# Three starts of stages rearranged in a 15-stage vision tower: buffers cleared behind the gathers, maxima of q, k and v taken one pair later, the shared experts' weights loaded in the routing before them

## The chip, the cores and the metric

The kernel runs on one core of one Trainium2 chip. The metric is the device time of one execution in microseconds; 2848.2 is the median of three runs. A profile is one more execution, recorded by the hardware.

## The reference, cut to what matters

The model is a tower of four layers over 64 images of 36 tokens (2304 tokens of width 192, f32). Each layer is an attention-like block and a feed-forward block, each followed by a layer norm of `h + block(h)`. Three blocks matter here:

```python
def L2_attn(x, ...):                       # "spectral"
    z = causal_conv4(x @ W_mem)            # 4 taps: the token and the 3 before it
    k_val, s_raw = z[..., :192], z[..., 192:]
    q = x @ W_q
    p_w = exp(clip(score_scale * s_raw, -20, 20) - slopes * dist)
    phi = tanh(tanh_scale * k_val) * theta            # 192 x 4 angles
    sums = cumsum([p_w, k_val * p_w * cos(phi), k_val * p_w * sin(phi)])
    ...                                    # times q and w_int, per-head products, gate
    return y @ out_W

def L2_ffn(x, ...):                        # swiglu: 2 shared experts, 16 routed, top 2
    shared = mean_s(silu(x @ shared_wg[s]) * (x @ shared_wu[s]) @ shared_wd[s])
    w, idx = top_k(softmax(x @ gate_w.T), 2)
    routed = sum_e combine[:, e] * (silu(x @ wg[e]) * (x @ wu[e]) @ wd[e])
    return shared + routed

def L3_attn(x, w_in, w_out):               # quantised: fake_quant needs the largest |value| of a whole tensor
    q, k, v = split(x @ fake_quant(w_in).T)
    q, k, v = fake_quant(q), fake_quant(k), fake_quant(v)
    scores = fake_quant(q @ k.T / 4)
    attn = fake_quant(softmax(scores))
    ...
```

## The kernel before

The tokens are held as 22 tiles of 108 (three images each), two tiles to a pair, so most loops run over 11 pairs (`NP = 11`, `G = 2`). The state `h` stays in SBUF. The program is a row of 15 stages (`PARTS`). In a stage every engine runs its own instruction list, written out by hand, with semaphores between engines; at the end of a stage all engines meet. The order within a list is fixed, so an instruction that waits holds up all behind it on that engine.

**Loading ahead.** `Ahead` reserves the SBUF of a later stage's weights and puts their transfers on the list `cst["coming"]`. A stage that calls `load_ahead` issues the whole list on SP's queue. The reader calls `arrived`, which waits until all transfers that were ever issued in this way have come. `clear_before` clears the semaphores of the stage before, one instruction for each, on SP. The routing stage of the swiglu block (`rt_swiglu`, `make_route`) does not call `load_ahead`; the next stage, `stage_shared`, loads its own weights `w1[x]`, `w2[x]` first and then the list: the quantised stage's three small tensors and `w2swiglu`, the 9216 KB of the routed experts.

**stage_shared.** TensorE runs `rise(n)` (up-projections) and `fall(n)` (down-projection) for 2 x 11 pairs. `rise` waits for `s_w[x]`, the two transfers of expert `x`. GpSimd meanwhile scatters the rows of `h` for the routed experts with 44 indirect transfers.

**Combine.** The stage behind a routed block gathers each token's expert rows by indirect transfers and adds and normalises them. For pair `p`: `fetch(2p)`, `fetch(2p+1)` on GpSimd (two gathers each, a ring of 4 tile buffers), `take(p)` on VectorE (two adds and statistics for each tile), `power(p)` on GpSimd (1/sqrt of the variances, and the shift), `level(p)` on ScalarE.

**stage_spectral.** GpSimd clears `hs` (the transposed pair and its three shifted copies, the borders of which must be zero, and one row of ones for the gate's bias) and `zz`. `shifts(p)` makes the shifted copies, `angles(p)` the angles `phi`, `scales(p)` the weights `kw`, `sums(p)` the sums of products. ScalarE's first copy into `hs` waits for `s_fix` = 3, the third clearing. TensorE's `keys(0)` waits for `shifts(0)`. VectorE's `rotations(0, u)` waits for `scales(0)` and ScalarE's sines; `weighted(0)`, which feeds `scales(0)`, comes ahead of `take(2)` on VectorE.

**stage_quantised, first phase.** For each pair TensorE projects q, k and v, ScalarE does `turned(p + 1)`, `level(p + 2)`, `queries(p)`, `values(p)` in this order, and VectorE `take(p + 2)`, `keys(p)` (copies k out of PSUM) and `looks(p)`: the largest absolute value of `h`, then of q (waits for `queries(p)`), k and v. When all 11 pairs are through, the scales of q, k, v are made, and the scores follow. `sel` is a constant bf16 matrix built from the identity, first needed after the scores; `q3` is the scores' left operand, whose borders must be zero. GpSimd clears both after the first 8 gathers, and VectorE fills `sel` between `take(0)` and `take(1)`:

```python
C_.take(dve, 0)
dve.wait_ge(s_fix, 4)
for i in range(3):
    dve.tensor_copy(sel[:, i]..., ident[0:T, i * IMG:(i + 1) * IMG]...)
C_.take(dve, 1)
for p in range(NP):
    if p + 2 < NP:
        C_.take(dve, p + 2)
    keys(p)
    looks(p)
```

## Time and profile before

| what | value |
|---|---|
| median of three runs | 2848.2 us (2841.95 to 2851.45) |
| profiled execution | 2844.44 us, span of its instructions 2842.6 us |
| TensorE busy | 2283.0 us, 80% of the span; mean granted clock 0.853 |
| VectorE, ScalarE, GpSimd busy | 1468.1, 895.3, 893.9 us |
| DMA | 225.44 MB, mean 79 GB/s |
| spectral stage | from about 1250 to 1661 us |
| routing of swiglu, shared experts, routed experts | 1661 to 1713, 1713 to 1965, 1966 to 2324 us |
| quantised stage | 2325 to 2619 us |

The profile counts from the first instruction. An engine is busy while it runs an instruction; "idle before <-releaser" is the time that it stood still before one, and what it had waited for last. PE is TensorE, DVE VectorE, ACT ScalarE, POOL GpSimd; SPq is SyncE's queue, which issues transfers. The granted clock is the share of full speed that TensorE got (1.00 is 2.4 GHz, 0.50 is 1.2 GHz).

### The profile page before, as it was taken

How to read it: one execution, taken by the hardware profiler on the slowest of the kernel's cores; microseconds unless marked ns; L12 is line 12 of the kernel's file. 1: busy time of each engine (PE TensorE's matmuls, PEld its weight loads, DVE VectorE, ACT ScalarE, POOL GpSimd, SP SyncE). 2: the span in 40 equal slices, each digit the busy share in tenths (PEclk: the TensorE clock that was granted, in tenths of full speed). 3: DMA queues.
4: the chain of work that ended last, by engine and by line, in shares of the span. 5: the costliest groups of instructions: out<-in, count | busy, mean ns of one | idle time of the engine just before them, and what ended most of it. 6: DMA issues, size and time to landing. Idle time of an engine off the chain costs nothing. (4 is left out here: it accounts for less than half of the span.)

```text
span 2842.6 us, 47911 instructions
## 1 busy us (share of the span) xinstructions
PE 2283.0 (80%) x18049; PEld 2006.4 (71%) x18049; DVE 1468.1 (52%) x3564; ACT 895.3 (31%) x1923; POOL 893.9 (31%) x809
## 2 busy tenths in 40 slices
PE   7999975599699759956888967998999977553793
PEld 7888863477588649954666667998999966532692
DVE  2667766456577632237888852222442236846313
ACT  0333326423154213324454411111111113754112
POOL 0332325600110342245665406000111136443424
PEclk9989975599799769977999968999999988555696
DMA  9500000060000435530000006001666631000453
GB/s 258 169 1 1 1 1 18 12 201 2 1 2 2 142 103 173 176 95 15 10 10 5 1 2 244 1 1 75 214 213 213 208 124 41 1 1 2 168 176 90
DMA packets 127066, 225.44 MB, mean 79 GB/s; under 512 B 17201, under 2 KB 97645, under 8 KB 119798
## 3 DMA queue, kind: packets, MB, share of 16 engines
q1 hardware_dynamic: 116278, 204.09, 21.9%
q0 software_dynamic: 10560, 18.29, 2.2%
q8 instruction: 145, 2.38, 0.3%
q14 instruction: 83, 0.68, 0.1%
HBM read 169.29 MB, written 53.02 MB: 78 GB/s over the span
## 5 line engine op out<-in xcount | busy, mean ns | idle before, releaser
L2513 POOL COPY bl_swiglu_w<-ahead_w2swiglu_w 128x1152 f32 x53 | 60.7, 1148 | 478.0 <-PE psum L2557 275.4
L2539 PE MATMUL psum<-bl_swiglu_xt,bl_swiglu_w 128*128 128x128 f32 x1272 | 153.0, 277 | 4.6 <-DMA bl_swiglu_w<-in_swiglu_w 3.6
L2539 PEld LDWEIGHTS psum<-bl_swiglu_xt,bl_swiglu_w 128*128 128x128 f32 x1272 | 151.0, 194 | 5.2 <-DMA bl_swiglu_w<-in_swiglu_w 4.0
L2581 ACT ACTIVATE bl_swiglu_sg<-psum 128x384 f32<-128x384 f32 x106 | 52.0, 490 | 310.5 <-PE psum L2546 310.5
L2608 DVE COPY bl_swiglu_xt<-psum 128x256 f32<-128x256 f32 x53 | 22.5, 424 | 206.5 <-PE psum L2524 206.5
L2692 PE MATMUL psum<-tower_xT,shared_w 128*128 128x216 f32 x528 | 103.1, 353 | 18.9 <-DMA shared_w<-in_shared_w 18.9
L2593 ACT ACTIVATE bl_gelu_hid<-psum,bl_gelu_w 128x128 f32<-128x128 f32 x270 | 74.5, 375 | 124.4 <-PE psum L2546 124.4
L2692 PEld LDWEIGHTS psum<-tower_xT,shared_w 128*128 128x128 f32 x528 | 98.5, 195 | 19.7 <-DMA shared_w<-in_shared_w 19.1
L2557 PE MATMUL psum<-bl_swiglu_w,bl_swiglu_hid 128*128 128x192 f32 x636 | 112.1, 326 | 0.0
L2737 DVE TENSOR_TENSOR shared_hid<-shared_sg,psum 128x432 f32<-128x432 f32 x66 | 39.9, 604 | 134.1 <-ACT shared_sg L2728 128.6
L2513 POOL COPY bl_gelu_w<-ahead_w2gelu_w 128x1350 f32 x45 | 58.9, 1312 | 152.5 <-DVE bl_gelu_y L2628 137.2
L2036 POOL DMA_INDIRECT rows_in<-tower_h,tower_spots x66 | 65.3, 990 | 122.5 <-POOLq L2094 74.8
L2557 PEld LDWEIGHTS psum<-bl_swiglu_w,bl_swiglu_hid 128*128 128x128 f32 x636 | 102.1, 190 | 0.1
L2728 ACT ACTIVATE shared_sg<-psum 128x432 f32<-128x432 f32 x66 | 35.0, 530 | 207.3 <-PE psum L2699 207.3
L2605 DVE TENSOR_SCALAR bl_gelu_xt<-psum,bl_gelu_gb 128x128 f32<-128x128 f32 x90 | 32.8, 406 | 121.5 <-PE psum L2524 121.5
L2557 PE MATMUL psum<-bl_gelu_w,bl_gelu_hid 128*128 128x192 f32 x540 | 95.3, 326 | 0.0
L2894 POOL TENSOR_TENSOR sp_pr<-sp_pr 108x768 f32<-108x768 f32 x44 | 78.5, 1812 | 42.2 <-DVE sp_pr L3196 42.2
L2711 PE MATMUL psum<-shared_w,shared_hid 128*108 128x192 f32 x528 | 91.1, 329 | 0.0
L2711 PEld LDWEIGHTS psum<-shared_w,shared_hid 128*108 128x108 f32 x528 | 84.5, 173 | 5.6 <-DVE shared_hid L2737 5.6
L2557 PEld LDWEIGHTS psum<-bl_gelu_w,bl_gelu_hid 128*128 128x128 f32 x540 | 86.9, 190 | 0.1
L2546 PE MATMUL psum<-bl_swiglu_xt,bl_swiglu_w 64*128 64x128 f32 x1272 | 85.3, 280 | 0.0
L2546 PEld LDWEIGHTS psum<-bl_swiglu_xt,bl_swiglu_w 64*128 64x128 f32 x1272 | 75.1, 187 | 6.4
(690 smaller groups left out, 6177.8 us busy)
## 6 DMA issues: line engine op xcount, KB each, us to landing
bl_swiglu_w<-in_swiglu_w SPq DMA_DIRECT2D x53, 1152.0 KB, 5.2
rows_in<-tower_zeros SPq DMA_DIRECT2D x2, 14592.0 KB, 48.0
bl_gelu_w<-in_gelu_w SPq DMA_DIRECT2D x45, 576.0 KB, 3.8
bl_relu_w<-in_relu_w SPq DMA_DIRECT2D x26, 576.0 KB, 3.8
ahead_w2swiglu_w<-in_swiglu_w SPq DMA_DIRECT2D x1, 9216.0 KB
tok_x<-in_x SPq DMA_DIRECT2D x11, 648.0 KB, 12.2
ahead_w2gelu_w<-in_gelu_w SPq DMA_DIRECT2D x1, 5400.0 KB
bl_swiglu_xr<-rows_in SPq DMA_DIRECT2D x53, 96.0 KB, 1.9
```

The costliest lines, as they stand in the source:

```text
L2036: pool.indirect_dma_start(out=cst["xs"], out_offset=at, in_=rows[:, t, :], in_offset=None).then_inc(cst["sent"], 16)
L2513: pool.tensor_copy(w2[:, n % DEEP], w2all[:, e, :].rearrange("p e n -> p (e n)")).then_inc(s_w2, 1)
L2539: pe.matmul(up_tile(n, j, i, side), w[:, o:o + 128], xt[:, n % 2, side, :], start=(i == 0), stop=False, skip_group_check=True)
L2546: ins = pe.matmul(up_tile(n, j, i, side), w[r, o:o + 128], xt[r, n % 2, 1 - side, :], start=False, stop=True, skip_group_check=True)
L2557: ins = pe.matmul(dn[:, n % 2, 0:D], hid[:, n % 2, k, :], w2[:, n % DEEP, k * D:(k + 1) * D], start=(k == 0), stop=(k == KC - 1))
L2581: act.activation(sg[:, j], bank_pair(n, j)[:, 0, 0:3 * BLOCK].rearrange("p (i n) -> p i n", i=3), ACT.Silu).then_inc(s_silu, 1)
L2593: ins = act.activation(hid[:, n % 2, m, :], up_tile(n, j, i, side), ACT.Gelu, bias=w2[:, n % DEEP, 6 * D + m:6 * D + m + 1])
L2692: pe.matmul(up[j][:, part * 2 + i, 0:C], w[:, o:o + 128], xT[:, part, cols], start=(i == 0), stop=False, skip_group_check=True)
L2711: ins = pe.matmul(dn[0:T, b, u, 0:D], hid[:, b, k, u * T:(u + 1) * T], w2[x][:, k, :], start=(k == 0), stop=(k == KC - 1))
L2728: act.activation(sg[:, j], up[j][:, 0:2, 0:C], ACT.Silu).then_inc(s_silu, 1)
L2737: dve.tensor_tensor(hid[:, n % 2, 2 * j:2 * j + 2, :], sg[:, j], up[j][:, 2:4, 0:C], ALU.mult).then_inc(s_hid, 1)
L2894: pool.tensor_tensor(pr[:, u, part, 0], pr[:, u, part, 0], pr[:, u, part, 1], op).then_inc(g_add, 1)
```

## The change

Three groups of edits. (1) The shared experts' weights become an `Ahead` of the swiglu routing, which now calls `load_ahead`; new transfers go to the head of the list instead of its end (this holds for all stages, and reverses the lists of the other three); `rise` waits for one semaphore that `arrived` sets. (2) In the spectral stage GpSimd clears only the borders of `hs` and sets only the ones that are read, takes `power(0)` ahead of `fetch(1)`, and `fetch(2)` and `power(2)` change places with `zz`, `shifts(0)` and `angles(0)`. (3) In the quantised stage `sel` and `q3` are cleared after the gathers and powers, VectorE fills `sel` in the second turn of the scores, and the maxima of q, k and v are taken one pair later.

```diff
 class Ahead:  __enter__
-            self.cst["coming"] += dmas
+            self.cst["coming"] = dmas + self.cst["coming"]
 make_route, sync
                     S.clear_before(sp)
-                    if kind != "swiglu":
-                        S.load_ahead(sp)
+                    S.load_ahead(sp)
+SHARED = 2
+def weights_shared(S, A):
+    w1 = [S.sb(f"w1{x}", [128, 3 * 768]) for x in range(SHARED)]
+    w2 = [S.sb(f"w2{x}", [128, 6, D]) for x in range(SHARED)]
+    return (w1, w2), [pair for x in range(SHARED) for pair in (
+        (w1[x][:], A["shared_w1"][x]), (w2[x][:].rearrange("p k n -> p (k n)"), A["shared_w2"][x]))]
 stage_shared, sync
+                S.arrived(sp, s_w)
                 S.clear_before(sp)
-                for x in range(N):
-                    sp.dma_start(w1[x][:], A["shared_w1"][x]).then_inc(s_w[x], 16)
-                    sp.dma_start(w2[x][:]..., A["shared_w2"][x]).then_inc(s_w[x], 16)
-                S.load_ahead(sp)
 stage_shared, rise
-                    pe.wait_ge(s_w[x], 32)
+                    pe.wait_ge(s_w, 1)
 stage_spectral, gpsimd
                 fetch(0)
+                for b in range(2):
+                    hi = hs[0:CH, b].rearrange("p s k (g n) -> p s k g n", n=IMG)
+                    for s in range(1, 4):
+                        ins = pool.memset(hi[:, s, :, :, 0:s], 0.0)
+                F_.then(ins)
+                F_.then(pool.memset(hs[CH:CH + 1, :, 0, 1, :], 1.0))
+                C_.power(pool, 0)
                 fetch(1)
-                F_.then(pool.memset(hs[0:CH], 0.0))
-                F_.then(pool.memset(hs[CH:CH + 1], 1.0))
-                C_.power(pool, 0)
-                fetch(2)
                 F_.then(pool.memset(zz[:], 0.0))
                 shifts(0)
+                fetch(2)
                 C_.power(pool, 1)
                 fetch(3)
+                C_.power(pool, 2)
                 pool.wait_ge(s_theta, 1)
                 angles(0)
-                C_.power(pool, 2)
                 fetch(4)
                 scales(0)
 stage_quantised, gpsimd
                 for t in range(WAY):
                     C_.fetch(pool, t)
-                pool.memset(sel[:], 0.0).then_inc(s_fix, 1)
-                pool.memset(q3[:], 0.0).then_inc(s_fix, 1)
                 for p in range(NP):
                     C_.power(pool, p)
                     if p + 2 < NP:
                         C_.fetch(pool, 2 * p + 4)
                         C_.fetch(pool, 2 * p + 5)
+                pool.memset(q3[:], 0.0).then_inc(s_fix, 1)
+                pool.memset(sel[:], 0.0).then_inc(s_fix, 1)
 stage_quantised, vector
                 def looks(p):
                     dve.wait_ge(C_.leveled, G * p + G)
                     largest(tm[0:T, 3, p:p + 1], tiles(h, p)).then_inc(s_tm, 1)
+
+                def looks_made(p):
                     dve.wait_ge(c_q, p + 1)
                     largest(tm[0:CH, 0, p:p + 1], q[:, :, pair(p)]).then_inc(s_tm, 1)
...
                 C_.take(dve, 0)
-                dve.wait_ge(s_fix, 4)
-                for i in range(3):
-                    dve.tensor_copy(sel[:, i]..., ident...)
                 C_.take(dve, 1)
                 for p in range(NP):
                     if p + 2 < NP:
                         C_.take(dve, p + 2)
                     keys(p)
                     looks(p)
+                    if p:
+                        looks_made(p - 1)
+                looks_made(NP - 1)
...
                 for p in range(NP):
                     if p + 1 < NP:
                         whole(p + 1)
+                    if p == 1:
+                        for i in range(3):
+                            dve.tensor_copy(sel[:, i]..., ident...)
                     dve.wait_ge(c_s, G * p + 2)
                     largest(tm[0:T, 4, p:p + 1], scored(p)).then_inc(s_tm, 1)
```

## Rows read from the trace of the kernel before

**Rows 1.** Windows, shared stage: us, busy per engine (instructions), granted TensorE clock, DMA share, GB/s.

```profile
1718.00:1722.00 4.00, 0.18 (x1) 0.18 (x2) 0.00 (x0) 0.00 (x0) 3.09 (x4) 0.50 0.99 391
...
1726.00:1754.00 28.00, 28.00 (x185) 26.30 (x184) 6.32 (x12) 4.77 (x9) 21.30 (x23) 0.97 1.03 403
...
1756.00:1758.00 2.00, 2.00 (x12) 1.74 (x10) 0.00 (x0) 0.00 (x0) 1.44 (x2) 1.00 0.52 180
```

**Rows 2.** Timelines of SP, ScalarE, TensorE: start, us, what, [idle before <-releaser].

```profile
1665.26 0.42 SPq L2100 DMA_DIRECT2D rt_swiglu_steps<-in_steps  x1
...
1712.77 1.28 ACT L2728 ACT_TABLE_LOAD   x1 [9.42 <-PEq L2094]
...
1718.13 0.48 SPq L116 DMA_DIRECT2D ahead_w2swiglu_w<-in_swiglu_w  x1
...
1721.82 7.58 PE L2692 MATMUL psum<-tower_xT,shared_w 128*128 128x216 f32 x24 [18.92 <-DMA shared_w<-in_shared_w]
```

**Rows 3.** Timeline of GpSimd (POOL), start of the spectral stage.

```profile
1255.40 1.00 POOL L2319 DMA_INDIRECT sp_got<-rows_out,tower_slots  x1 [0.31 <-issue]
...
1262.14 3.00 POOL L2903 MEMSET sp_hs<- 96x3456 f32 x1
...
1268.26 0.73 POOL L2354 TENSOR_TENSOR sp_cr<-sp_cvt,tower_half 108x2 f32<-108x2 f32 x1
...
1296.27 3.26 POOL L2879 TENSOR_TENSOR sp_phi<-sp_theta,sp_th 108x768 f32<-108x768 f32 x2 [11.24 <-ACT sp_th L3068]
...
1301.23 0.85 POOL L2354 TENSOR_TENSOR sp_cr<-sp_cvt,tower_half 108x2 f32<-108x2 f32 x1 [1.70 <-DVE sp_cvt L2342]
...
1307.64 3.06 POOL L2887 TENSOR_TENSOR sp_kw<-sp_wint,sp_kv 108x768 f32<-108x768 f32 x2
```

**Rows 4.** Timelines of VectorE and ScalarE in the same stretch.

```profile
1259.69 0.17 DVE L2341 TENSOR_SCALAR sp_cvt<-sp_cmv 108x2 f32<-108x2 f32 x1
...
1276.75 0.51 ACT L3059 COPY sp_hs<-psum 96x432 f32<-96x432 f32 x1 [6.47 <-POOL sp_zz L2907]
...
1296.10 2.03 DVE L2327 SCALAR_TENSOR_TENSOR tower_h<-sp_got,tower_gates,tower_h 108x192 f32<-108x192 f32 x2
```

**Rows 5.** Timeline of GpSimd, first phase of the quantised stage.

```profile
2336.19 1.19 POOL L3397 MEMSET qa_sel<- 108x1296 bf16 x1
...
2337.30 2.99 POOL L3398 MEMSET qa_q<- 96x3456 bf16 x1
...
2340.25 0.75 POOL L2354 TENSOR_TENSOR qa_cr<-qa_cvt,tower_half 108x2 f32<-108x2 f32 x1
...
2346.59 0.73 POOL L2354 TENSOR_TENSOR qa_cr<-qa_cvt,tower_half 108x2 f32<-108x2 f32 x1
...
2352.80 0.74 POOL L2354 TENSOR_TENSOR qa_cr<-qa_cvt,tower_half 108x2 f32<-108x2 f32 x1
...
2402.48 0.72 POOL L2354 TENSOR_TENSOR qa_cr<-qa_cvt,tower_half 108x2 f32<-108x2 f32 x1 [1.12 <-DVE qa_cvt L2342]
...
2409.48 0.69 POOL L2354 TENSOR_TENSOR qa_cr<-qa_cvt,tower_half 108x2 f32<-108x2 f32 x1 [6.00 <-DVE qa_cvt L2342]
```

**Rows 6.** Timeline of VectorE in the same phase.

```profile
2337.41 3.15 DVE L3835 CAST qa_sel<-tower_ident 108x108 bf16<-108x108 f32 x3 [2.56 <-POOL qa_sel L3397]
...
2376.47 1.11 DVE L3715 TENSOR_REDUCE qa_tm<-qa_qk 96x1 f32<-96x432 f32 x2 [1.58 <-ACT qa_qk L3589]
...
2396.96 0.60 DVE L3730 COPY qa_qk<-psum 96x432 f32<-96x432 f32 x1 [1.85 <-PE psum L3447]
...
2399.42 0.86 DVE L2327 SCALAR_TENSOR_TENSOR tower_h<-qa_got,tower_gates,tower_h 108x192 f32<-108x192 f32 x2
...
2415.05 0.60 DVE L3730 COPY qa_qk<-psum 96x432 f32<-96x432 f32 x1 [1.59 <-PE psum L3447]
```

**Rows 7.** Windows, one pair of the quantised first phase (columns as in rows 1).

```profile
2360.60:2367.70 7.10, 5.74 (x25) 4.89 (x26) 5.00 (x16) 2.17 (x5) 5.00 (x7) 0.76 0.19 50
```

**Rows 8.** Timeline of TensorE in the scores of the quantised stage.

```profile
2438.87 1.33 PE L3471 MATMUL psum<-qa_kz,qa_q 32*108 32x72 bf16 x36 [1.18 <-DVE qa_kz L3750]
```

More of the change, by code:

```diff
@@ L2646, in make_blocks @@
     return stage_blocks
+SHARED = 2
[4 more added lines that the diff above has]
+        (w1[x][:], A["shared_w1"][x]), (w2[x][:].rearrange("p k n -> p (k n)"), A["shared_w2"][x]))]
 def stage_shared(nc, A, h, cst):
     HID, KC = 768, 6
-    N = 2
+    N = SHARED
     xT, side = cst["xT"], cst["side"]
     with Stage(nc, "shared", cst) as S:
-        w1 = [S.sb(f"w1{x}", [128, 3 * HID]) for x in range(N)]
-        w2 = [S.sb(f"w2{x}", [128, KC, D]) for x in range(N)]
+        w1, w2 = cst["ahead"]["shared"]
         hid = S.sb("hid", [128, 2, KC, C])
@@ L2661, in stage_shared @@
         dn = S.ps([128, 2, 2, 256])
-        s_w = S.sems("w0", "w1")
-        s_up, s_silu, s_hid, s_dn, s_acc = S.sems("up", "silu", "hid", "dn", "acc")
+        s_w, s_up, s_silu, s_hid, s_dn, s_acc = S.sems("w", "up", "silu", "hid", "dn", "acc")
         with nc.Block() as block:
@@ L2667, in _ @@
             def _(sp):
+                S.arrived(sp, s_w)
                 S.clear_before(sp)
-                for x in range(N):
-                    sp.dma_start(w1[x][:], A["shared_w1"][x]).then_inc(s_w[x], 16)
-                    sp.dma_start(w2[x][:].rearrange("p k n -> p (k n)"), A["shared_w2"][x]).then_inc(s_w[x], 16)
-                S.load_ahead(sp)
             @block.gpsimd
@@ L3832, in _ @@
                 C_.take(dve, 0)
-                dve.wait_ge(s_fix, 4)
-                for i in range(3):
-                    dve.tensor_copy(sel[:, i].rearrange("p (j n) -> p j n", n=144)[:, :, 0:IMG],
-                                    ident[0:T, i * IMG:(i + 1) * IMG].unsqueeze(1).broadcast_to([T, 3, IMG]))
                 C_.take(dve, 1)
@@ L3857, in _ @@
                         whole(p + 1)
+                    if p == 1:
+                        for i in range(3):
+                            dve.tensor_copy(sel[:, i].rearrange("p (j n) -> p j n", n=144)[:, :, 0:IMG],
+                                            ident[0:T, i * IMG:(i + 1) * IMG].unsqueeze(1).broadcast_to([T, 3, IMG]))
                     dve.wait_ge(c_s, G * p + 2)
@@ L3958, in expert_layer @@
 def expert_layer(kind):
-    shared = [stage_shared] if kind == "swiglu" else []
-    return [make_route(kind)] + shared + [make_blocks(kind)]
+    first = [make_route(kind)]
+    if kind == "swiglu":
+        first = [([("shared", weights_shared)], first + [stage_shared])]
+    return first + [make_blocks(kind)]
 def resident(kind):
```

## Prediction

> **What bounds the kernel now.** I read the page first, then the table of groups by line to find where each stage begins, then timelines by engine of the three places that the diff touches. The kernel is a string of 15 stages, each ended by a barrier of all engines, and the stages have different limits. The chain of waits on the page follows only the last stage back, so it says nothing about this change; each place is read from its own timeline.
>
> *Start of the shared experts.* In [rows 2] the shared stage opens at 1712.77, when ScalarE leaves the barrier. TensorE starts only at 1721.82, and what it waited for last is the transfer of `shared_w`. The 18.92 us of idle time shown there is longer than the loss, because TensorE had also nothing to do during the tail of the routing on VectorE. From then on TensorE is the bound: it is busy in 28.00 of the 28 us from 1726 on [rows 1].
>
> *Start of the spectral stage.* GpSimd does everything in one queue: 8 gathers, the clearing of `hs` (3.00 us, and then again about 3 us for its one constant row), and only then the first `power`, at 1268.26 [rows 3]. VectorE had the variances of pair 0 ready at 1259.69 plus 0.17 [rows 4]. ScalarE's first copy into `hs` waits for the third clearing, `zz`, until 1276.75 [rows 4]. So everything that follows hangs on GpSimd's order.
>
> *First phase of the quantised stage.* The clearings of `sel` and `q3` (1.19 and 2.99 us) stand ahead of the first `power` at 2340.25 [rows 5]. After that, `power` recurs every 6.21 us while nothing holds GpSimd up (2346.59 to 2352.80), but from there it takes 7.09 us per pair: 2352.80 to 2409.48 is 56.68 us for 8 pairs [rows 5]. The reason is a ring. VectorE waits 1.58 us for ScalarE's copy of q in each turn [rows 6]; ScalarE does that copy behind `level(p + 2)`, which waits for `power(p + 2)`, which waits for VectorE's `take(p + 2)`, which VectorE does after the maxima of q, k and v of the pair before. The ring is take, power, level, copy of q, maxima, take.
>
> **The change part by part.** All three are seen from the time of the profiled execution, 2844.4 us, which is 3.8 under the median of the three runs, 2848.2.
>
> *Shared weights in the routing.* Removed: 8 loads that SP issued from 1714.26 on (the last, `w2swiglu`, at 1718.13 [rows 2]). Added: the same 8 in `rt_swiglu`, behind its own small loads, of which the last is issued at 1665.26 [rows 2], and behind the clearing of the spectral stage's 52 semaphores. The clearing of routing's 17 took from 1712.77 to 1714.26, so 52 take 3 to 5 us: the loads go out from about 1670. They are 3456 KB shared, 9216 KB `w2swiglu` and 625 KB for the quantised stage, 13.6 MB. In the shared stage they ran with the scattered rows beside them until the DMA share halves in 1756 to 1758 [rows 1], 43 us after the first issue. At that pace they are done by 1713, and at the 403 GB/s of [rows 1] without the scatter in 34 us, by 1704. TensorE needs all of them now, not only the first two, since `arrived` counts the whole batch; it can start at about 1713.4. So the work that hides them is the routing on VectorE, some 43 us of it, and the cover is 0.4 to 9 us thick. Gain 1721.8 - 1713.4 = **8.4 us**; for each microsecond that the batch is late beyond 1713.4, one less. Nothing queues behind SP's wait but its clearing of semaphores. TensorE starts at its lower clock, 1.2 GHz (granted 0.50 in 1718 to 1722 [rows 1]), after 19 us of idling; after 10 it should be no other, so the slow first group (7.58 us [rows 2]) stays. The reversed order of the lists in the other three stages that load ahead changes no total: every reader there waits for the whole batch. Cost 0, bounds 1 us either way.
>
> The Trainium skill (DMA: Bandwidth & Descriptors, section Where 436 GB/s comes from) puts the limit of a load from HBM at about 358 GB/s for a core. By it the 13.6 MB would take 38 us and be there by 1708, and the sum would be the same; the trace shows 403 GB/s, though that counts the scatter too.
>
> *Spectral start.* GpSimd's fourth gather ends at 1256.40 [rows 3]. The six small clearings of 12 to 36 elements per partition and one of 432 on one partition stand for two of 3456. No such small one is in the rows; by the rate of the large ones (3.00 us for 3456) plus a start they come to 1 to 1.5 us, with 0.5 and 3 as bounds. All of these are under the 3.5 us until the variances are there, so they cost nothing, and `power(0)` starts at 1259.93 in place of 1268.26: 8.33 earlier. Behind it stand the same four gathers and `zz` as before, so `zz`, ScalarE's copy, the shifts and the matmuls come 8.33 us earlier too. The gathers of pair 1 are some 4 us later than before and land near 1269; VectorE needs them only before `keys(0)`, ten microseconds later.
>
> Then something is given back. `power(2)` now stands ahead of `angles(0)`, and it waits for `take(2)`, which VectorE starts at 1296.10 [rows 4], so at 1287.8 after the shift. A take with GpSimd idle is 3.06 us (2399.42 to the `power` at 2402.48 [rows 5, 6]), so `power(2)` starts at 1290.9, ends at 1292.0, and `angles(0)` runs to 1295.3. The four gathers of pair 4 are 5.3, and `scales(0)` starts at 1300.6, against 1307.64 [rows 3]. Before, `angles(0)` ran first (1296.27, 3.26 us), then GpSimd waited 1.70 for `take(2)` [rows 3], which it had itself slowed down. So of 8.3 us, **7.0 us** arrive at `scales(0)`, from which VectorE's rotations and the main loop follow. Bounds 5 (small clearings dear, or ScalarE late) and 8.3.
>
> *Quantised start.* `power(0)` moves from 2340.25 to 2336.2, as do the next gathers: 4.0 us. VectorE no longer sits 2.56 + 3.15 us over `sel` [rows 6] ahead of `take(1)`, but that was inside GpSimd's time already. With the maxima one pair later, the copy of q that they want is long made, and the ring is longer by one turn: from `power(p)` to `keys(p - 1)` 5.57 us (2409.48 to 2415.05), then from `keys` through all maxima and a take to `power(p + 2)` 5.52 us (2396.96 to 2402.48) [rows 5, 6]. That is 11.09 for two pairs, 5.55 each, so it is under GpSimd's own 6.21, and GpSimd becomes the bound. The last `power` comes 6 x 6.21 + 11.09 = 48.4 us after `power(2)` instead of 56.7: 8.3 us less. TensorE's lower clock appears in some pairs (mean 0.76 in one [rows 7], where its busy time is 5.74 us of 7.10) and stretches the ring; I take off 1.6 and keep 6.7. Bounds: 8.3, and 1 if the lower clock holds in most pairs. At the end the maxima of two pairs stand behind the last keys in place of one: 1.5 us back. The clearings of `q3` and `sel`, 4.2 us, now lie after the last `power`, where GpSimd has nothing to do until the scales are ready.
>
> The three casts into `sel` now fall into the scores, where TensorE waits 1.18 us per pair for VectorE [rows 8], so they are on the path. They took 3.15 us under a clearing by GpSimd [rows 6]; GpSimd works beside them here too, in shorter instructions. Between 0 and 3.15 I take 1.0. Sum: 4.0 + 6.7 - 1.5 - 1.0 = **8.2 us**.
>
> The Trainium skill (SBUF — State Buffer, section Who interferes with whom) says that a VectorE cast in a two-port mode and a GpSimd instruction share a pair of ports as an exclusive lock, so that the second waits for the whole of the first. The row agrees: 2.9 of the 3.15 us are the clearing of `q3`. By the rule the casts would wait for one of GpSimd's roundings, about a microsecond.
>
> **Sum.** 8.4 + 7.0 + 8.2 = 23.6 us: the profiled execution comes to 2820.8, and the median to 2848.2 - 23.6 = **2824.6**. A difference of 0.3%, 8.5 us, is what a measurement of this kernel can tell from none.
>
> **Rivals.**
> 1. *TensorE takes GpSimd's place as the bound of the quantised loop.* The denser loop keeps falling to the lower clock, pairs stay near 7 us, and that stage brings 4.0 + 1 - 1.5 - 1.0 = 2.5. For it: the clock of 0.76 [rows 7]. Against: the clock fell there after TensorE had waited for `level`, and these waits get shorter. Time 2848.2 - 17.9 = 2830.
> 2. *The spectral start gives back more.* `power(2)` ahead of `angles(0)` costs a further 4 us since ScalarE or GpSimd is held up elsewhere. Time 2829.
> 3. *The batch is late.* `arrived` waits for 13.6 MB, and the routing is the cover. If the loads run at 300 GB/s, they take 45 us and end 2 us late: 2826.5. It ends on the other side when the batch comes more than 23.6 us after 1713.4, at 1737: that takes a rate under 203 GB/s. In [rows 1] they moved at twice that. Time then 2848 or above.
> 4. *The change doesn't do what it says.* The loads moved could hold up the routing's own small loads; they stand ahead in SP's queue, so no. All gains as forecast but the ring stays: this is rival 1.
>
> **Chances and range.** Forecast 0.62, rival 1 0.18, rival 2 0.10, late but still faster 0.05, slower side of it 0.02, more gain than forecast 0.03. Range: all bounds kind give 8.4 + 8.3 + 10.8 = 27.5, plus 1 for the order of the lists and the spread of three runs, which reaches 6 us under their median: 2815. All unkind without late loads: 7.4 + 5 + 0.4 = 12.8, so 2835.4, rounded to 2836. Faster by more than 0.3%: 0.93; within: 0.05; slower: 0.02.
>
> **What would show it.** In the profile after: TensorE's first shared matmul waits for no transfer and starts under 1 us after ScalarE's table load there; `power(0)` of the spectral stage within 0.3 us of the variances, and `scales(0)` about 45.2 us after the start of the stage's fourth gather (52.2 before [rows 3]); in the quantised stage the `power` of GpSimd every 6.2 to 6.5 us, VectorE without its wait of 1.58 us for q, and `sel` cast in 1 to 2 us. The prediction is wrong if TensorE waits on SP's count, if pairs stay at 7 us, or if a microsecond gained at a stage's start is lost in its loop.

## The result, and the profile after

The changed kernel takes 2824.97 us (median of 4 runs, 2820.97 to 2829.91) against 2848.53 for the kernel before (4 runs), a ratio of 0.9921 with a 95% interval of 0.9894 to 0.9948. The forecast was 2824.6 in a range of 2815 to 2836. So the total came out almost to the microsecond, but not the terms: two were too small and one was too large. Such closeness is luck: the four runs fall into two pairs, near 2829 and near 2821, with the median between them, and the interval of the ratio stands for a gain of 15 to 30 us. The profiled execution of the changed kernel took 2829.91 us, where the forecast for it was 2820.8; its span is 2828.1.

**Shared experts.** Timelines of SyncE's queue, ScalarE and TensorE in the changed kernel, at the end of the swiglu routing:

```profile
1669.12 0.42 SPq L2100 DMA_DIRECT2D rt_swiglu_steps<-in_steps  x1
...
1672.57 1.97 SPq L116 DMA_DIRECT2D ahead_shared_w<-in_shared_w  x4
1674.58 0.47 SPq L116 DMA_DIRECT2D ahead_w2swiglu_w<-in_swiglu_w  x1
1675.10 16.28 SPq L116 DMA_DIRECT2D ahead_qa_wi<-in_qa_wi  x1
...
1716.66 1.28 ACT L2733 ACT_TABLE_LOAD   x1 [9.42 <-PEq L2094]
...
1716.72 6.55 PE L2697 MATMUL psum<-tower_xT,ahead_shared_w 128*128 128x216 f32 x24 [9.93 <-SPq L123]
```

And the windows over the routing (stretch, us, busy time of TensorE, granted clock, DMA share, GB/s):

```profile
1680.00:1706.00 26.00, 21.63 (x103) 0.50 1.02 411
1706.00:1710.00 4.00, 0.59 (x2) 0.50 0.65 136
1710.00:1716.00 6.00, 0.00 (x0) 0.50 0.00 0
```

TensorE starts 0.06 us after ScalarE opens the stage; in [rows 2] it was 9.05 us. The releaser named, SPq L123, is the `arrived` of the stage: SyncE had it at once, since the transfers had ended some 8 us before, between 1708 and 1709. The first group of 24 matmuls takes 6.55 us instead of 7.58. The issue of `qa_wi` holds SyncE's queue for 16.28 us, now that it stands behind the 9216 KB of `w2swiglu` (0.49 in the kernel before, where it stood ahead of them), so the last load is issued only at 1695.01. It costs nothing here, because the whole batch is there in time.

**Spectral start.** GpSimd in the changed kernel:

```profile
1262.98 0.40 POOL L2910 MEMSET sp_hs<- 96x12 f32 x6
1263.44 0.45 POOL L2912 MEMSET sp_hs<- 1x432 f32 x1
...
1266.67 0.73 POOL L2353 TENSOR_TENSOR sp_cr<-sp_cvt,tower_half 108x2 f32<-108x2 f32 x1 [2.78 <-DVE sp_cvt L2341]
...
1298.56 0.84 POOL L2353 TENSOR_TENSOR sp_cr<-sp_cvt,tower_half 108x2 f32<-108x2 f32 x1 [8.56 <-DVE sp_cvt L2341]
...
1299.63 3.18 POOL L2884 TENSOR_TENSOR sp_phi<-sp_theta,sp_th 108x768 f32<-108x768 f32 x2
...
1308.11 3.05 POOL L2892 TENSOR_TENSOR sp_kw<-sp_wint,sp_kv 108x768 f32<-108x768 f32 x2
```

The stage starts at 1257.7 here and at 1251.1 before, so 6.6 us are to be taken off when these rows are laid beside [rows 3]. The small clearings of `hs` cost 0.85 us in all. The first `power` waits for VectorE, no longer the reverse. `power(2)` waits 8.56 us, and `angles(0)` stands behind it. `scales(0)` comes 6.1 us earlier against the stage's start.

**Quantised first phase.** GpSimd's `power` of pairs 2, 3 and 10 and the clearing behind it, and the window between the first and the last of these (the engines' busy times in the order TensorE, its weight loads, VectorE, ScalarE, GpSimd):

```profile
2342.00 0.73 POOL L2353 TENSOR_TENSOR qa_cr<-qa_cvt,tower_half 108x2 f32<-108x2 f32 x1
2348.26 0.73 POOL L2353 TENSOR_TENSOR qa_cr<-qa_cvt,tower_half 108x2 f32<-108x2 f32 x1
...
2390.80 0.70 POOL L2353 TENSOR_TENSOR qa_cr<-qa_cvt,tower_half 108x2 f32<-108x2 f32 x1 [3.92 <-DVE qa_cvt L2341]
...
2391.70 2.97 POOL L3411 MEMSET qa_q<- 96x3456 bf16 x1
```

```profile
2342.00:2390.80 48.80, 38.86 (x230) 34.19 (x229) 40.68 (x117) 17.49 (x40) 36.30 (x45) 1.00 0.19 50
```

The same eight pairs took 56.68 us in the kernel before [rows 5]. Its window over them, to be read beside this one:

```profile
2352.80:2409.48 56.68, 47.09 (x239) 40.37 (x237) 42.45 (x121) 17.79 (x40) 35.87 (x44) 0.88 0.16 43
```

TensorE was busy 8.2 us less, for 230 matmuls against 239 in the window: its clock did not fall once in it.

In the scores, TensorE waits for VectorE ahead of each group. The groups of the second and third pair, in the changed kernel and then in the kernel before:

```profile
2416.39 1.33 PE L3480 MATMUL psum<-qa_kz,qa_q 32*108 32x72 bf16 x36 [2.08 <-DVE qa_kz L3761]
2420.07 1.33 PE L3480 MATMUL psum<-qa_kz,qa_q 32*108 32x72 bf16 x36 [2.35 <-DVE qa_kz L3761]
```

```profile
2433.82 1.33 PE L3471 MATMUL psum<-qa_kz,qa_q 32*108 32x72 bf16 x36 [2.42 <-DVE qa_kz L3750]
2436.35 1.34 PE L3471 MATMUL psum<-qa_kz,qa_q 32*108 32x72 bf16 x36 [1.20 <-DVE qa_kz L3750]
```

The wait of the third grows from 1.20 to 2.35 us, since the casts stand ahead of it; that of the second was no shorter before (2.42, now 2.08).

**All stages.** The length of each stretch in us, from the first instruction on one tile of a stage to the first of the next, in every profile taken. mlstm is the recurrence of the first layer (five other stretches lie between it and the spectral stage, so its length bears on the total alone); "shared" runs from the start of the swiglu routing to the first SiLU of the shared experts; "scales" from the start of the quantised stage to the first rounding of v; "rest" from there to its end.

| kernel | mlstm | spectral | shared | scales | rest |
|---|---|---|---|---|---|
| before | 375.7 | 410.7 | 68.6 | 100.8 | 194.1 |
| changed | 383.1 | 408.0 | 58.5 | 90.3 | 194.7 |
| e1_shared | 378.8 | 410.7 | 59.0 | 101.8 | 194.1 |
| e2_spectral | 379.5 | 404.7 | 68.6 | 100.9 | 194.0 |
| e3_quantised | 376.4 | 410.7 | 68.8 | 90.1 | 194.7 |
| e4_order | 380.7 | 410.8 | 68.7 | 100.9 | 194.0 |
| e5_again | 380.9 | 409.6 | 59.4 | 90.3 | 194.8 |
| e6_angles_first | 384.5 | 403.6 | 59.1 | 90.2 | 194.8 |
| e7_not_delayed | 378.3 | 408.0 | 58.6 | 98.7 | 194.7 |
| e8_casts_last | 376.6 | 407.9 | 58.6 | 90.2 | 194.1 |
| e9_all | 380.9 | 397.2 | 58.7 | 88.7 | 194.1 |
| e10_angles_tail | 373.8 | 403.7 | 59.1 | 88.7 | 194.1 |
| e11_spectral_again | 380.2 | 407.4 | 70.7 | 100.7 | 194.1 |

### The profile page after: what moved, and what is told of

The parts are those of the page before. It is cut to its first block and busy times, and to the rows that moved or that the text cites. A ratio compares the mean times of both kernels' runs of the same rounds, so it can differ in the third digit from the quotient of the medians.

```text
span 2828.1 us, 47916 instructions
## 1 busy us (share of the span) xinstructions
PE 2286.7 (81%) x18049; PEld 2010.3 (71%) x18049; DVE 1469.2 (52%) x3564; ACT 894.9 (32%) x1923; POOL 888.5 (31%) x814
## 5 line engine op out<-in xcount | busy, mean ns | idle before, releaser
L2607 DVE COPY bl_swiglu_xt<-psum 128x256 f32<-128x256 f32 x53 | 22.5, 425 | 206.0 <-PE psum L2523 206.0
L2697 PE MATMUL psum<-tower_xT,ahead_shared_w 128*128 128x216 f32 x528 | 102.1, 351 | 9.9 <-SPq L123 9.9
L2697 PEld LDWEIGHTS psum<-tower_xT,ahead_shared_w 128*128 128x128 f32 x528 | 97.6, 194 | 10.6 <-SPq L123 10.1
L2716 PE MATMUL psum<-ahead_shared_w,shared_hid 128*108 128x192 f32 x528 | 91.1, 330 | 0.0
L2716 PEld LDWEIGHTS psum<-ahead_shared_w,shared_hid 128*108 128x108 f32 x528 | 84.5, 173 | 5.6 <-DVE shared_hid L2742 5.6
```

The source lines that it names most:

```text
L2697: pe.matmul(up[j][:, part * 2 + i, 0:C], w[:, o:o + 128], xT[:, part, cols], start=(i == 0), stop=False, skip_group_check=True)
L2716: ins = pe.matmul(dn[0:T, b, u, 0:D], hid[:, b, k, u * T:(u + 1) * T], w2[x][:, k, :], start=(k == 0), stop=(k == KC - 1))
```

## The experiments

The kernels from e5 on ran on two other chips, on which the kernel before takes 2894.92 and 2895.96 us (medians), so they are read by their ratio to it and by the table.

### Each part alone: e1 to e4

e1 is the kernel before with only the shared experts' loads moved, e2 with only the changed order of GpSimd's spectral queue, e3 with only the quantised part, e4 with only this line:

```
-            self.cst["coming"] += dmas
+            self.cst["coming"] = dmas + self.cst["coming"]
```

> The kernel before with the shared experts' weights loaded in the swiglu routing, and nothing else (the load lists keep their old order). Theory (each part acts in its own stage, and the parts add): from the start of the swiglu routing to the first SiLU of the shared stage 10.1 us less than before, 9.05 from the missing wait and 1.0 from a shorter first group of matmuls; no other stage moves by more than 1.5 us except by TensorE's clock; the time is 10 us less, 2838. Rival (the loads take something back from the routing or from the resident weights behind it): under 8 us are left at the start of the swiglu blocks, and the routing's own steps on VectorE, 5.70 to 5.78 us apart before, come further apart.

> The kernel before with the spectral start changed, and nothing else. Theory A (the gain of the start is real and passes through the loop; the 3.4 us that the changed kernel lost in the loop were a matter of where TensorE's clock fell in that one execution): the copies of the keys by VectorE come 29.2 or 31.2 us apart in all pairs, with up to 2.5 us added only in pairs in which the granted clock falls under 0.95, TensorE's first running sums come 6.1 us earlier against the start of the stage, and the time is 6 us less, 2842. Theory B (the earlier gathers or the new order cost something in the loop): pairs 2 and 7 of the loop are again 1.5 and 0.8 us longer than before at the same granted clock, the stage gains under 3.5 us, and the time is 3 us less, 2845.

> The kernel before with the quantised first phase changed, and nothing else (clearings behind the powers, maxima of q, k and v one pair later, casts into sel in the scores). Theory (GpSimd's own 6.21 us per pair is the bound once the maxima are late): the powers come 6.2 us apart in all pairs, the first rounding of v comes 10.5 us earlier against the start of the stage, 1 us of it is lost in the scores, and the time is 9.5 us less, 2838.7. Rival (TensorE's clock bounds the loop, and the changed kernel was lucky in the one execution seen): pairs of 6.6 to 7.1 us appear where the granted clock is under 0.9, and the gain is 3 to 7 us.

> The kernel before with the load lists put in the reverse order, and nothing else. Theory (every reader waits for the whole batch, so the order costs nothing, and the 7.4 us by which the stage of the matrix-memory recurrence (mlstm) was longer in the changed kernel's profile are chance, from where TensorE's clock fell): the time is within 3 us of before, 2845 to 2851, and the mlstm stage is 375.7 or some 7 us more, whichever, in executions of both kernels. Rival (the order matters there): the mlstm stage is 383 us again, and the time is 5 to 7 us above before, 2854.

| kernel | median, us | ratio to before (2849.94) | 95% interval |
|---|---|---|---|
| e1_shared | 2838.46 | 0.9963 | 0.9952 to 0.9975 |
| e2_spectral | 2844.99 | 0.9980 | 0.9969 to 0.9990 |
| e3_quantised | 2838.48 | 0.9971 | 0.9960 to 0.9981 |
| e4_order | 2846.96 | 0.9993 | 0.9980 to 1.0006 |

The parts are worth 10.5, 5.7 and 8.3 us by their ratios, 24.5 together; the whole change gave 0.0079 x 2850 = 22.5. They act in their own stages and add, within what can be measured. For e1 and e3 the theory held, with 9.6 us in the shared stretch (10.1 forecast) and 10.7 at the quantised scales (10.5 forecast). For e2 the time decides nothing, since its interval, 3 to 9 us, holds both theories; by its profile the stage gained 6.0, as theory A had it, and e11 below takes that back. For e4 the rival is excluded: the time is not 5 to 7 us above. The order of the lists cannot be told from no change. Its mlstm stage, 380.7, lies in the spread of that stage over all thirteen profiles, 373.8 to 384.5; the mean of the five with the old order is 378.1, of the eight with the new 379.9. So nothing shows that the 7.4 us by which that stage was longer in the first profile of the changed kernel are from this change; of all stretches between marks it is the one that varies most.

### The spectral loop: e5, e6, e10, e11

The start of the stage had brought 6.1 us, but the stage was only 2.7 shorter; e2 suggested that the missing 3.4 were chance. e5 is the changed kernel again, and e11 is e2 again. e6 puts one call back where it was, on top of the changed kernel:

```
-                C_.power(pool, 2)
                 pool.wait_ge(s_theta, 1)
                 angles(0)
+                C_.power(pool, 2)
```

> The changed kernel once more, as it is. Theory (the 3.4 us lost in the spectral loop and the 7.4 us longer mlstm stage of its first profile are chance): the spectral stage, from the first gather to the start of the swiglu routing, takes 404.7 us, as it did with its part of the change alone, and not 408.0; the mlstm stage takes between 376 and 383; the time lies with the sum of the parts measured alone, 9.6 + 6.0 + 10.1 = 25.7 us under before, 2823 to 2825. Rival (the parts together cost something that no part costs alone): the spectral stage takes 408 again, and the time is 3 us above the sum of the parts.

> The changed kernel with GpSimd's power of pair 2 put back behind the angles of pair 0. My working (the power ahead of the angles holds them up until VectorE has taken pair 2, and so gives back some of the start's gain): the angles of pair 0 start at once when ScalarE's tanh is there, 2.8 to 4 us earlier against the start of the stage, the scales of pair 0 come 1.5 to 2.5 us earlier, and the time is 2 us less. Rival (ScalarE's level of pair 2 then stands between the angles and the sines, so the sines come when they came and VectorE's rotations too): the scales come earlier, the first rotation of VectorE does not move by more than 0.7 us, and the time is the same within 1 us.

> The kernel before with the spectral start changed, a second time. Theory (the power ahead of the angles brings the longer falls of the clock wherever it stands): intervals of 33.6, 34.8 and 30.9 us between copies of the keys, spectral stage 408 us. Rival (what the first look at it showed was no chance either): 32.0, 34.0 and 29.2 again, spectral stage 404.7 us.

e5 measured a ratio of 0.9918 (0.9894 to 0.9941), e6 0.9917 (0.9894 to 0.9941); e11 has one time, 2893.58 us, and is read by its profile. The copies of the keys by VectorE mark the pairs of the loop. Their distances in us:

| order at the start | kernels | distances |
|---|---|---|
| before | before, e1, e3, e4 | 41.1 29.1 32.0 31.2 31.2 32.1 32.0 33.9 29.2 29.2 |
| power, then angles | changed, e5, e7, e8, e11 | 41.7 29.1 33.6 32.0 31.2 31.2 32.0 34.8 29.2 30.9 |
| power, then angles | e2 | 41.9 29.1 32.0 31.2 32.0 32.1 31.2 34.0 29.2 29.2 |
| angles, then power | e6, e10 | 41.2 29.1 32.0 31.2 31.2 32.1 32.0 33.9 29.2 29.2 |
| angles, then power, all of it earlier | e9 | 39.7 29.1 31.2 32.0 31.2 31.2 32.1 34.8 29.2 30.9 |

(Within a row of this table the kernels differ by at most 0.15 us in any place.) My theory for e5 (chance) was wrong: the loss is the same in five executions on three chips. Its rival had the loss right but not the reason, a cost of the parts together, since e11 has the spectral part alone and the same loss. Windows of the changed kernel's third distance, of three places in it and one in the next, and of the tenth, TensorE alone:

```profile
1357.60:1391.23 33.63, 29.86 (x128) 0.90 0.04 11
...
1377.70:1380.70 3.00, 1.22 (x2) 0.76 0.22 55
1380.70:1383.70 3.00, 3.00 (x6) 0.50 0.00 0
1383.70:1386.70 3.00, 3.00 (x10) 0.60 0.00 0
1408.70:1414.70 6.00, 3.77 (x10) 0.89 0.19 42
...
1581.68:1612.59 30.91, 28.25 (x128) 0.94 0.01 1
```

The same places in e10, which has the angles first:

```profile
1351.76:1383.81 32.05, 28.29 (x128) 0.95 0.04 11
...
1372.40:1375.40 3.00, 1.75 (x4) 0.76 0.13 35
1375.40:1378.40 3.00, 3.00 (x9) 0.67 0.00 0
1378.40:1381.40 3.00, 3.00 (x19) 1.00 0.00 0
1403.40:1409.40 6.00, 3.10 (x10) 1.00 0.11 28
...
1573.46:1602.70 29.24, 26.58 (x128) 1.00 0.01 1
```

Each has 128 matmuls in the long windows. A mean of 0.76 over 3 us stands for 1.4 us at 0.50, so the three windows have 6.8 us at the lower clock in the one and 3.4 in the other. At half speed 3.4 us more cost 1.7 of work, and the distance is 1.6 us longer. In the tenth distance the clock falls in the one and not in the other, for 1.7 us. (The fall in the next distance is no loss: in e10 it comes two distances later, and costs 0.9 us in either place.) With 0.8 in the eighth this is 4.1, of which 0.7 were made up elsewhere between the first running sums and the end of the stage. So the loss is TensorE's clock. Two things go with it. One is the order at the stage's start: in the changed kernel, e7 and e10 the clock rises in the first keys at the same 26.0 us after the stage's start, and e10, with the angles first, does not have the loss. The other is the time of this rise, since e2 and e11 are the same program with different distances: it is 26.7 us in e2, 25.4 in e11 and 25.9 in e5, as windows show, e2, e11 and then e5:

```profile
1282.40:1283.40 1.00, 1.00 (x6) 0.64 0.30 83
```

```profile
1286.00:1287.00 1.00, 1.00 (x6) 0.78 0.10 37
```

```profile
1285.30:1286.30 1.00, 1.00 (x5) 0.56 0.32 78
```

The windows start 26.0, 25.0 and 25.0 us into the stage. That this shift of about a microsecond between the clock and the work decides over 3 us of loop is a reading of one exception; neither the shift nor what sets it was tried. Order alone does not settle it either, since e9 has the angles first and two of the three longer distances.

e6 itself: `angles(0)` starts 37.9 us into the stage instead of 41.9, `scales(0)` at 49.3 instead of 50.4, and TensorE's first running sums at 55.4 instead of 56.5. My 1.5 to 2.5 us were 1.1; the stage is 6.0 shorter than e5's and 4.3 shorter than e7's and e8's, so the larger part is the clock again. (e5's own stage is 1.6 us longer than e7's and e8's because the clock stayed low for 10.2 us at its end instead of 6.8.) The profiled execution of e6 was no faster than e5's because its mlstm stage and what lies ahead were 8.5 us longer; the medians were 2874.79 and 2874.92: the gain in the stage is shown, one in the time is not.

### What the quantised part is made of: e7, e8

e7 takes the maxima of a pair in its own turn again; the clearings and casts stay moved. e8 changes only when `sel` is filled:

```
-                    if p:
-                        looks_made(p - 1)
-                looks_made(NP - 1)
+                    looks_made(p)            # e7

-                    if p == 1:
+                    if p == NP - 1:          # e8
                         for i in range(3):
```

> The changed kernel with the maxima of q, k and v of a pair taken in its own turn again; the clearings and the casts stay where the change put them. My working (4.0 us of the gain are the clearings, the rest the ring): VectorE waits 1.5 us for q in each turn again, the powers come 6.8 to 7.1 us apart from the third on, the last of them 5.5 to 8.3 us later than in the changed kernel, the tail of the maxima is 1.5 us shorter, and the time is 5 to 6 us more. Rival (the clearings were what had put the ring out of step; without them GpSimd's 6.21 us hold anyway): the powers stay at 6.2 us, and the time is 1.5 us less.

> The changed kernel with VectorE's three casts into sel made in the last pair of the scores, where VectorE waited 1.03 us for ScalarE, instead of the second. My working (the casts are on the path of the scores and cost 1.0): the gap of TensorE ahead of the third pair's scores falls from 2.35 to 1.2 us, the stage's score phase is 1 us shorter, and the time 1 us less. Rival (VectorE catches up within the later pairs, where it is not the bound): the gap goes, but the last scores come at the same time within 0.3 us.

e7 measured 0.9949 (0.9933 to 0.9966), 9 us more than the changed kernel beside it, where I had 5 to 6. The ring is back, and the rival is excluded. GpSimd and VectorE in e7:

```profile
2402.34 0.72 POOL L2353 TENSOR_TENSOR qa_cr<-qa_cvt,tower_half 108x2 f32<-108x2 f32 x1 [0.88 <-DVE qa_cvt L2341]
...
2409.39 0.73 POOL L2353 TENSOR_TENSOR qa_cr<-qa_cvt,tower_half 108x2 f32<-108x2 f32 x1 [0.88 <-DVE qa_cvt L2341]
```

```profile
2425.97 1.11 DVE L3724 TENSOR_REDUCE qa_tm<-qa_qk 96x1 f32<-96x432 f32 x2 [1.16 <-ACT qa_qk L3598]
```

The powers are 7.05 us apart, and the last of them is 8.2 us later against the stage's start than in e5 (80.6 against 72.5). The phase is 8.4 us longer, more than my 5.5 to 8.3 less 1.5, because TensorE's clock also fell in the last pair (0.77 in the 7.4 us from 2444.60 on): its 16 projections of q and k took 4.65 us there and 3.08 in the kernel before. Its last power still stands 3.9 us before that of the kernel before: this is the clearings' share.

e8 measured 0.9926 (0.9900 to 0.9953), too wide to tell 1 us from 0.9918. Its rest of the stage takes 194.1 us, as before the change, against 194.7 to 194.8 in all kernels with the casts in the second pair. So the casts cost 0.6 to 0.7 us there and nothing in the last pair, less than my 1.0 and more than the 0.3 of the rival. TensorE's third group and VectorE's casts in e8:

```profile
2461.25 1.33 PE L3480 MATMUL psum<-qa_kz,qa_q 32*108 32x72 bf16 x36 [1.20 <-DVE qa_kz L3761]
...
2478.72 0.49 DVE L3869 CAST qa_sel<-tower_ident 108x108 bf16<-108x108 f32 x3
```

The casts take 0.49 us with GpSimd idle. In the changed kernel they took 1.12 beside GpSimd's roundings:

```profile
2415.73 0.98 POOL L3416 TENSOR_SCALAR tower_side<-tower_side,qa_rc 108x384 f32<-108x384 f32 x1
2416.26 1.12 DVE L3869 CAST qa_sel<-tower_ident 108x108 bf16<-108x108 f32 x3
```

The rounding under way ends 0.45 us after the casts begin, and they take 0.63 us more than alone. By the rule of the Trainium skill (SBUF — State Buffer, section Who interferes with whom) a cast in a two-port mode waits for the whole of a GpSimd instruction that has the shared ports. The rows agree with it, and do not prove a lock.

### A better version: e9, e10

e10 is e6 with the casts of e8, and with the maxima of the last pair but one taken while VectorE waited for TensorE's last keys. e9 has these two changes of the quantised stage and a new start of GpSimd's spectral queue. The maxima (in both) and the queue (in e9):

```
+                    if p == NP - 1:
+                        looks_made(p - 1)
                     keys(p)
                     looks(p)
-                    if p:
+                    if 0 < p < NP - 1:
                         looks_made(p - 1)
...
                 F_.then(pool.memset(hs[CH:CH + 1, :, 0, 1, :], 1.0))
+                F_.then(pool.memset(zz[:], 0.0))
                 C_.power(pool, 0)
-                fetch(1)
-                F_.then(pool.memset(zz[:], 0.0))
+                C_.fetch(pool, 2)
                 shifts(0)
+                C_.fetch(pool, 3)
...
-                C_.power(pool, 2)
                 pool.wait_ge(s_theta, 1)
                 angles(0)
+                C_.power(pool, 2)
+                scales(0)
                 fetch(4)
-                scales(0)
```

> The changed kernel with GpSimd's spectral start in another order (zz cleared in the 2.8 us that GpSimd waited ahead of the first power; the shifts of pair 0 between the two tiles of pair 1; then angles, power of pair 2 and scales ahead of the gathers of pair 4), the casts into sel in the last pair of the scores, and the maxima of the last pair but one ahead of the last copy of the keys. My working: ScalarE's copy of pair 0 and the shifts come 5.5 us earlier, the copy of the keys too, the scales a further 2 to 5 us, so TensorE's first running sums come 8 to 10 us earlier; in the quantised stage 1.6 us at the end of the maxima and 0.7 in the scores. Sum 10 to 12 us under the changed kernel, ratio to before 0.988. Rival (VectorE's own work between the copy of the keys and the sines, or TensorE's clock, takes it): under 5 us.

> The changed kernel with the angles ahead of the power of pair 2, the casts in the last pair of the scores, and the maxima of the last pair but one ahead of the last copy of the keys. Theory (the length of the clock's falls in the spectral loop follows from the order at its start, not from chance): the copies of the keys come 41.1, 29.1, 32.0, 31.2, 31.2, 32.1, 32.0, 34.0, 29.2 and 29.2 us apart, as they did with the angles ahead, and the spectral stage takes 403.6 us. Rival (chance): intervals of 33.6, 34.8 and 30.9 appear again and the stage takes over 406. In the quantised stage the scales come 1.6 us earlier against its start and the scores take 0.7 less; the whole is 3 to 6 us under the changed kernel.

e9 takes 2863.6 us against 2895.96, a ratio of 0.9890 (0.9870 to 0.9910); e10 0.9903 (0.9882 to 0.9925). GpSimd in e9 (the stage starts at 1257.2):

```profile
1263.48 2.26 POOL L2913 MEMSET sp_zz<- 128x2592 f32 x1
1266.26 0.72 POOL L2353 TENSOR_TENSOR sp_cr<-sp_cvt,tower_half 108x2 f32<-108x2 f32 x1 [0.51 <-DVE sp_cvt L2341]
...
1293.71 0.85 POOL L2353 TENSOR_TENSOR sp_cr<-sp_cvt,tower_half 108x2 f32<-108x2 f32 x1 [1.70 <-DVE sp_cvt L2341]
1294.78 3.19 POOL L2892 TENSOR_TENSOR sp_kw<-sp_wint,sp_kv 108x768 f32<-108x768 f32 x2
```

The clearing of `zz` fills the wait ahead of the first `power`, the scales stand 12.8 us earlier than in the changed kernel (37.6 us into the stage, not 50.4), and the first running sums 12.0 us earlier, more than my 8 to 10. The stage takes 397.2 us, 10.8 less than in the changed kernel's first profile. The quantised stage gives 1.6 in its first phase and 0.6 in the scores, as in e10. In its loop e9 still has the eighth and tenth distance of the longer kind, 34.8 and 30.9. My 10 to 12 us under the changed kernel are 13.0 by the stages of the profiles, and by ratios 0.9890 against 0.9921 and 0.9918, so 8 to 9 us, with intervals that overlap: likely faster than the changed kernel, and faster than the kernel before without doubt. e10 is 4 to 5 us under it by ratios (3 to 6 forecast), which the intervals do not set apart from 0. It brought the old distances back a second time, as the theory had it.

## Why the prediction was right, and where it was not

The total was right because three errors cancelled: by the table the three stretches gave 10.1 + 2.7 + 9.9 = 22.7 us in the first profile, where I had 8.4 + 7.0 + 8.2 = 23.6. The profiled execution was only 14.5 us shorter, since the mlstm stage took 7.4 us more and the last routed experts 2.3 more, neither of which any run ties to the change. That the median showed nearly the whole sum is luck in part.

**Shared weights, 8.4: right mechanism, 10.1 measured (9.6 in e1).** The loads had 8 us of cover, near the thick end of my 0.4 to 9; so TensorE did not have to wait for 1713.4 but started with the stage, 9.0 us earlier instead of 8.4. The rest is the first group of matmuls, which I had left at 7.58 us and which took 6.55, since the clock rose sooner in it. Rival 3, the late batch, did not occur: 411 GB/s against the 203 at which it would have decided. This is more than the 358 GB/s that the Trainium skill (DMA: Bandwidth & Descriptors, section Where 436 GB/s comes from) gives for loads from HBM; here no scatter ran beside them, which was the reserve I had made. The transfers ended 35 to 36 us after the first issue, against 34 by the rate of [rows 1] and 38 by that figure.

**Spectral start, 7.0: the term that failed.** Up to the scales the working holds: `power(0)` 8.2 us earlier (8.33 forecast), `scales(0)` 6.1 (7.0 forecast), 46.1 us after the start of the fourth gather where I wrote 45.2. The missing 0.9 arose ahead of ScalarE's first copy, which came 7.5 us earlier instead of 8.33: the second instruction of `power(0)` took 0.45 us (0.20 before), and the next two gathers 1.29 and 1.25 (1.08 and 1.00 before), perhaps because VectorE works beside them now, which no run tested. Between that copy and `scales(0)` 1.3 us are given back, as forecast for `power(2)`; e6, which moves it back, wins 1.1. The step that failed is "from which VectorE's rotations and the main loop follow", and the sentence in which 7.0 us "arrive": the loop lost 3.4 of the 6.1. That is rival 2 in its size (4 us more given back), but not in its cause, which I had put on ScalarE or GpSimd; it is TensorE's clock. By the last sign that I had named for a wrong prediction, a microsecond gained at a stage's start and lost in its loop, this term was wrong; I had no price for it.

**Quantised start, 8.2: right mechanism, 9.9 measured (10.1 in e3).** `power(0)` came 4.1 us earlier (4.0), the eight pairs took 48.80 us (48.4) against 56.68, so the ring is worth 7.9, not the 6.7 that I kept after an allowance of 1.6 for the clock; the tail of the maxima cost 1.5 (1.5); the casts cost 0.6 (1.0). e7 shows that it is the delay of the maxima that undoes the ring, and not the moved clearings. Rival 1, TensorE's clock as the bound of the quantised loop, was wrong in its sign: with the waits gone from the ring the clock stayed at 1.00 over the eight pairs (0.88 before).

**Order of the lists, 0 (plus or minus 1): not told apart from 0.** e4's interval, -5.7 to +1.7 us, is wider than my bounds.

## What to carry to other kernels

Take a gain at the head of a loop as the gain of the stage only when the turns behind it have kept their lengths; where TensorE's clock falls and rises in the loop, they may not. Here 6.1 us at the head were 2.7 at the end, and the same edit with one call in another place gave 7. A ring over several engines is best opened by taking one consumer a turn later, if the turn's other work is then the bound; work out the time around the longer ring over the number of turns in it (5.55 us here), and take the next bound where that is longer (GpSimd's 6.21). It gave 48.4 us here against 48.80 measured. Read parts of a sum by stage marks over several profiles, since single runs of this kernel differ by as much as each part brings (2841 to 2856 us for the kernel before on one chip).

## What the runs showed of the hardware

**The pattern of clock falls repeats.** The distances between pairs agree within 0.15 us over executions, chips and programs that differ elsewhere, but two patterns exist for nearly the same program, 4.1 us apart over the third, eighth and tenth distance. The order at the start goes with the switch from one to the other (e10 against the changed kernel), and so does the time at which the clock rises (e2 against e11); which of them decides, and how, is open.

**On two of the chips TensorE stood idle for most of a stretch of the shared stage.** Windows of 15 us in it, TensorE alone, first the changed kernel on its first chip, then e5 and then e11 on others:

```profile
1760.00:1775.00 15.00, 15.00 (x104) 1.00 0.22 67
```

```profile
1760.00:1775.00 15.00, 2.87 (x6) 0.50 0.20 61
```

```profile
1760.00:1775.00 15.00, 3.70 (x11) 0.61 0.38 136
```

The timeline of e5 there:

```profile
1763.58 0.48 PE L2716 MATMUL psum<-ahead_shared_w,shared_hid 128*108 128x192 f32 x1 [2.32 <-issue]
1766.37 0.48 PE L2716 MATMUL psum<-ahead_shared_w,shared_hid 128*108 128x192 f32 x1 [2.32 <-issue]
```

Single matmuls come up to 2.8 us apart, and "issue" says that no semaphore or transfer in the profile held them. In e5 it begins some 10 us after the first of GpSimd's 44 scatters of this stage, which are issued 1.29 us apart on all chips, and ends some 5 us after the last. From the first SiLU of the shared experts to the start of the routed ones it is 281.2 us in e5 against 235.6 on the first chip, so it costs some 45 us, and 38 in e11, which has the old shared stage; the kernel before is 45 us slower on these chips. Because its end seems set by the scatters, moving TensorE's start forward brings less there: from the start of the routing to the end of the shared stage it is 344.4 us in e11 and 338.2 and 339.0 in e9 and e10 on the same chip, so 5.4 to 6.2 instead of 9.6 to 10.1. Whether the instructions themselves come late was not tested.
